# Token statistics taken in the convolution stage, and gate rows written from ScalarE's queue, in a four-layer image network

## Chip, core and metric

The kernel runs on one core of a Trainium2 chip. The metric is the time of one execution on the device, in microseconds (us); less is better. The engines are TensorE (PE: matrix products and transposes), VectorE (DVE), ScalarE (ACT), GpSimd (POOL) and SyncE (SP, which here only issues transfers). Each runs its own instruction stream in order; they meet at semaphores.

## What is computed

An image batch x of shape (4, 64, 128, 128), fp32, goes through four layers, each a mixing block over the image and a feed-forward block over its 65,536 tokens of 64 channels, both with a normalisation ahead and a residual around them. The change touches layer 1 (both blocks) and the feed-forward block of layer 3:

```python
x = x + L1_conv(_ln_c(x)); t = tokens(x); t = t + L1_ffn(_ln_t(t))
...
t = tokens(x); t = t + L3_ffn(_ln_t(t))          # same function, other weights

def L1_conv(x, gamma, beta, w_lbp, w_1x1, b_1x1):
    xn = batch_norm(x, gamma, beta)               # mean, variance over batch and image
    y = relu(conv3x3(xn, w_lbp)) + x
    return einsum('bchw,oc->bohw', y, w_1x1) + b_1x1

def ffn(x, router_w, router_b, expert_w, expert_b):   # 8 experts, 2 per token
    p, i = top_k(softmax(x @ router_w + router_b), 2)
    p = p / p.sum(-1)
    all = einsum('bnd,edc->bnec', x, expert_w) + expert_b
    return einsum('bnk,bnkc->bnc', p, take_along_axis(all, i))

def _ln_t(v):                                      # over the 64 channels of a token
    return (v - mean(v)) / sqrt(var(v) + 1e-5)
```

## The kernel before

build_program emits the stages one after another; each has its own on-chip tiles and one instruction stream per engine, and the next stage opens when all engines have ended. The names of tiles in the profile carry the stage's prefix.

**Convolution stage** (stage_conv_bn, prefix cb). Its first phase normalises all tokens and turns them to channel-major strips u. Its second walks 64 strips of 8 image rows in pairs. For each pair TensorE makes the 3x3 convolution (L1444, L1458); VectorE adds relu of it to u and writes y (add_relu, L1341 for the even strip, two halves L1345 for the odd); TensorE multiplies y by the 1x1 weights, which turns it back to tokens (mix, L1469); VectorE adds the old tokens, to which POOL has added the bias (L1263), into h (add_rest, L1353). SP loads old tokens (L1200) and stores new ones (L1205), a tile of 1024 tokens each, in the layout tokens_by_pair. mix of a pair comes a half pair after its convolution, between the next pair's straight and beside products. ScalarE normalises the strips ahead (L1401, L1404).

**Routed stage** (stage_top2_ffn, prefix t) runs twice: t1 in layer 1, where tiles of tokens are loaded from and stored to memory (rows is None), and t3 in layer 3, where the tokens lie on chip in passes and POOL joins a residual column to them (L1704) and the finished image is stored by SP in 32 pieces (L1655). Both make 32 beats; a beat works on four tiles in different steps. Its steps for a beat n: VectorE takes the statistics of n+3 (stats: 16 x L1727, five small operations), ScalarE their root (L1808, L1811), VectorE the shift (norm, L1739). ScalarE normalises n+2 (normalise, 2 x 8 x L1819), TensorE turns it (L1910), ScalarE copies it to ht (L1827), TensorE makes router logits and turns them (L1918, L1925), VectorE picks two experts (route, L1743 to L1759) and, after an exponential (L1841), makes the gates (gate, L1763 to L1768). TensorE turns the gates of n+1 (L1932), ScalarE copies them to gs (save_gates, L1837), SP writes them to memory as rows (keep_gates, L1634), and, when that has landed, SP reads each row back, spread to 64 partitions (spread_gates, 8 transfers of 512 KB into z, L1642). VectorE multiplies z by ht (weigh, L1775), TensorE sums over the experts (mix, L1942) and adds the residual (L1948, L1951), ScalarE copies out (finish, L1853), and SP stores (t1: L1647; t3: four times 8 image stores).

The order on ScalarE in a beat is written out: normalise(n+2, 0), save_gates(n+1), normalise(n+2, 1), copies of the turned halves, logits, root(n+3), mixed result, finish. The order on SP in a beat is load(n+4) (t1) or load_columns(2n+9) (t3), store(n-1), keep_gates(n+1), spread_gates(n+1, 0), load_columns(2n+10), spread_gates(n+1, 1). `since` waits for a semaphore only from a positive count on.

Of the kernel before, what the change touches and what calls it, by code (L numbers as in the profile page):

```python
# [1080 lines left out]
def stage_conv_bn(nc, tok, gamma, beta, w_lbp, w_1x1, b_1x1):  # L1081
# [8 lines left out]
    with ExitStack() as ctx:  # L1090
# [25 lines left out]
        y = a.sb("y", [128, 2, R, P2])  # L1116
        pH = [a.ps(f"pH{i}", [128, 512]) for i in range(2)]
# [34 lines left out]
        sum_ready = a.sem("sum_ready")  # L1152
        stored = [a.sem(f"stored{i}") for i in range(2)]
# [23 lines left out]
        def tokens_by_pair(n):  # L1177
            return tok[bass.ds(n * TILE, TILE), :].rearrange("(q p j) c -> p q (j c)", p=128, j=2)

        @block.sync  # L1180
        def _(sp):
# [16 lines left out]
            def load(n, par):  # L1198
                sp.wait_ge(sum_ready, n + 1)
                sp.dma_start(xs[:, par, :, :].rearrange("p (q j) c -> p q (j c)", j=2),  # L1200
                             tokens_by_pair(n)).then_inc(r_in[par], 16)

            def store(n, par):
                sp.wait_ge(sum_ready, n + 3)
                sp.dma_start(tokens_by_pair(n), h[:, par, :, :].rearrange(  # L1205
                    "p (q j) c -> p q (j c)", j=2)).then_inc(stored[par], 16)
# [62 lines left out]
        def _(dve):  # L1269
# [61 lines left out]
            def add_relu(n):  # L1331
# [30 lines left out]
        @block.scalar  # L1362
        def _(act):
# [43 lines left out]

            for n in range(B * NT):
                normalise(n)

# [93 lines left out]
def stage_top2_ffn(nc, stage, tok, router_w, router_b, expert_w, expert_b, gate_rows, rows=None, image=None):  # L1504
# [13 lines left out]
    with ExitStack() as ctx:  # L1518
# [91 lines left out]
        def _(sp):  # L1610
# [21 lines left out]
            def keep_gates(m):  # L1632
                sp.wait_ge(gs_saved, m + 1)
# [1224 lines left out]
```

## Time and profile before

| | |
|---|---|
| median of 3 runs | 6325.05 us (6322.73 to 6328.15) |
| profiled execution | 6345.72 us, its span 6343.9 us |
| busy in the span | PE 5095.5, DVE 4296.8, ACT 3437.0, POOL 1150.9 us |
| convolution stage, second phase | about 1456 to 1778 us |
| t1 | about 1782 to 2446 us |
| t3 | about 5563 to 6344 us |

All times on the time axis are from the start of the span of the one profiled execution. A timeline row begins with start and duration; "x8" joins eight like instructions that follow each other; a bracket holds the idle time of that engine before the row and what ended it. SPq is SP's queue issuing transfers; such a row's duration is the issue, not the transfer. PEclk is the TensorE clock that the throttle granted, 1.00 being full speed (2.4 GHz) and 0.50 the lower level (1.2 GHz). Instructions whose work is hidden beside another engine cost nothing; what counts in a stage is the wait that ends last.

### The profile page before, as it was taken

To read this page: it belongs to the slowest core of one execution; us is meant where nothing else is said; L and a number is where in the kernel's file an instruction comes from. 1 tells how busy PE (TensorE), PEld (TensorE's weight loads), DVE (VectorE), ACT (ScalarE), POOL (GpSimd) and SP (SyncE) were. 2 spreads that over 40 slices of the span, in tenths; PEclk is the share of its full clock that TensorE was granted. 3 is DMA by queue.
4 is the path that set the end of the run, shared out by engine and by line. 5 is a ranking of instruction groups with operands and counts; after the bars stand their busy time and mean duration, and the time that the engine had idled before them with its cause. 6 is when DMAs were issued, how large, how long until landed. Compare 5 with 4: busy or idle time off the path is not lost. (4 is left out here: it accounts for less than half of the span.)

```text
span 6343.9 us, 130904 instructions
## 1 busy us (share of the span) xinstructions
PE 5095.5 (80%) x47166; PEld 3310.4 (52%) x47166; DVE 4296.8 (68%) x9648; ACT 3437.0 (54%) x6857; POOL 1150.9 (18%) x1068
## 2 busy tenths in 40 slices
PE   7887886548968885799969998308999999948887
PEld 5665664224533332699969994104555555523332
DVE  7896887793358887622223447697777777768886
ACT  5664665465546564522243225366676767645554
POOL 2332332162200003400000000131111112221110
PEclk9998998758989996799989999659999999979999
DMA  1111113232358884200000124237666666547777
GB/s 35 36 32 35 37 37 84 67 104 83 108 164 277 276 281 159 69 0 0 0 0 0 67 102 132 66 98 96 81 81 81 81 81 81 68 137 238 238 241 223
DMA packets 794229, 646.31 MB, mean 102 GB/s; under 512 B 496551, under 2 KB 644199, under 8 KB 793779
## 3 DMA queue, kind: packets, MB, share of 16 engines
q1 hardware_dynamic: 792755, 639.06, 40.7%
q8 instruction: 307, 5.03, 0.3%
q0 software_dynamic: 1024, 1.05, 0.1%
q14 instruction: 143, 1.17, 0.1%
HBM read 549.78 MB, written 90.20 MB: 101 GB/s over the span
## 5 line engine op out<-in xcount | busy, mean ns | idle before, releaser
L2365 PE MATMUL sw_pC<-sw_row,sw_wc 128*128 128x128 f32 x10160 | 1159.3, 274 | 56.2 <-DVE sw_row L2240 54.9
L2365 PEld LDWEIGHTS sw_pC<-sw_row,sw_wc 128*128 128x128 f32 x10160 | 1148.0, 191 | 58.3 <-DVE sw_row L2240 55.5
L2799 PE MATMUL sp_pC<-sp_work,sp_bands 64*64 64x512 f32 (+11 forms) x14592 | 986.0, 428 | 44.2 <-issue 44.2
L2228 DVE SCALAR_TENSOR_TENSOR sw_row<-sw_pC,sw_y 128x128 f32<-128x128 f32 x1016 | 337.7, 332 | 792.2 <-PE sw_pC L2365 792.2
L2799 PEld LDWEIGHTS sp_pC<-sp_work,sp_bands 64*64 64x64 f32 x14592 | 602.1, 133 | 431.4 <-issue 365.3
L2738 ACT ACTIVATE sp_pC<-sp_pC,sp_par 128x512 f32<-128x512 f32 x832 | 598.4, 741 | 371.1 <-PE sp_pC L2799 348.0
L1775 DVE TENSOR_TENSOR t_z<-t_z,t_ht 128x1024 f32<-128x1024 f32 x512 | 628.4, 1267 | 93.8 <-DMA t_z<-gate_rows 91.7
L1942 PE MATMUL t_pO<-t_z,t_ew 128*64 128x512 f32 x2048 | 518.6, 626 | 100.0 <-DVE t_z L1775 98.3
L2297 ACT ACTIVATE sw_y<-sw_row 128x128 f32 (+1 forms) x762 | 265.6, 349 | 592.7 <-DVE sw_row L2228 592.7
L2695 DVE TENSOR_TENSOR sp_work<-sp_work,sp_pC 128x512 f32<-128x512 f32 x512 | 351.5, 688 | 170.1 <-ACT sp_pC L2738 169.6
L308 POOL TENSOR_TENSOR wa_sc<-wa_sc,wa_sm 128x1024 f32<-128x1024 f32 x128 | 243.8, 1904 | 665.7 <-DVE wa_sm L397 665.7
L1910 PE MATMUL t_pT<-t_ident,t_h 128*128 128x128 f32 x1024 | 158.5, 304 | 199.5 <-ACT t_h L1819 109.5
L1942 PEld LDWEIGHTS t_pO<-t_z,t_ew 128*64 128x64 f32 x2048 | 125.3, 139 | 349.0 <-DVE t_z L1775 185.5
L2738 ACT ACTIVATE sp_side<-sp_pC,sp_par 64x512 f32<-64x512 f32 x384 | 297.3, 774 | 7.5
L2600 POOL COPY sp_bands<-sp_bands 128x1536 f32<-128x1536 f32 x96 | 141.1, 1470 | 813.3 <-PE sp_pC L2799 774.6
L1910 PEld LDWEIGHTS t_pT<-t_ident,t_h 128*128 128x128 f32 x1024 | 125.7, 155 | 271.4 <-ACT t_h L1819 160.0
L2812 PE MATMUL sp_pC<-passes,sp_roll 128*128 128x512 f32 x128 | 59.0, 616 | 219.0 <-ACT passes L2729 219.0
L821 POOL MEMSET c_eps<- 128x1 f32 x2 | 0.2, 102 | 1256.0 <-POOLq L56 1256.0
L2693 DVE TENSOR_TENSOR sp_work<-sp_work,sp_pC 64x512 f32<-64x512 f32 x320 | 219.6, 686 | 7.1
L1704 POOL TENSOR_TENSOR passes<-passes,t_xs 128x512 f32<-128x512 f32 x64 | 118.1, 1846 | 558.1 <-DMA t_xs<-tokens 558.1
L1846 ACT ACTIVATE t_oc<-t_pO 128x512 f32<-128x512 f32 x128 | 76.3, 596 | 261.2 <-PE t_pO L1942 261.2
L2330 ACT ACTIVATE sw_packed<-sw_row 128x128 f32<-128x128 f32 x256 | 79.5, 311 | 249.2 <-DVE sw_row L2228 249.2
(375 smaller groups left out, 9736.8 us busy)
## 6 DMA issues: line engine op xcount, KB each, us to landing
t_z<-gate_rows SPq DMA_DIRECT2D x512, 512.0 KB, 8.0
sp_bands<-windows SPq DMA_DIRECT2D x128, 512.0 KB
c_spent<-tokens SPq DMA_DIRECT2D x128, 256.0 KB, 2.7
cb_xs<-tokens SPq DMA_DIRECT2D x128, 256.0 KB, 2.9
wa_xs<-in_x SPq DMA_DIRECT2D x64, 256.0 KB, 2.9
tokens<-wa_xt SPq DMA_DIRECT2D x128, 128.0 KB, 1.9
tokens<-cb_h SPq DMA_DIRECT2D x64, 256.0 KB, 2.7
t_xs<-tokens SPq DMA_DIRECT2D x32, 512.0 KB, 11.5
```

Of the source, the lines that this page charges most:

```text
L308: pool.tensor_tensor(p, p, r, ALU.mult).then_inc(probs_ready, 1)
L1775: dve.tensor_tensor(z[:, i, q, :], z[:, i, q, :], ht[:, m.k % HR, i, :], ALU.mult).then_inc(z_ready, 1)
L1910: ins = pe.transpose(pT[s][:, 128 * j:128 * j + 128], h[:, i, 4 * s + j, :, :].rearrange("p c d -> p (c d)"), ident[:, :])
L1942: ins = pe.matmul(pO[i][64 * s:64 * s + 64, :], ew[:, q, :], z[:, i, q, 512 * s:512 * s + 512], start=(q == 0), stop=(q == 3))
L2228: dve.scalar_tensor_tensor(row[par][c][:, :, PAD:PAD + P2], pC[c][:, 0:2 * P2].rearrange("p (b w) -> p b w", b=2), 0.0, line(sweep, c, i), ...
L2297: act.activation(line(sweep, c, i), row[par][c][:, :, PAD:PAD + P2], ACT.Copy).then_inc(saved[c], 1)
L2365: ins = pe.matmul(pC[c][:, 0:2 * P2], wc[:, sweep, m, :], row[1 - par][c][:, :, m:m + P2], start=(m == 0), stop=(m == 4))
L2600: pool.tensor_copy(dst, src[:, :, ::-1]).then_inc(band_ready, 1)
L2693: ins = dve.tensor_tensor(new[halves[here], :], old[halves[here], :], rel[halves[1 - here], :], ALU.add)
L2695: return dve.tensor_tensor(new, old, rel, ALU.add)
L2738: return act.activation(out[rows_out, :], pC[q][rows_in, :], ACT.Relu, bias=par[rows_in, c, BI + i:BI + i + 1], scale=par[rows_in, c, SC + ...
L2799: ins = pe.matmul(out[halves[to], :, low * lo:low * hi], band[halves[k], (NV * g + j) % BANDS, q, AT[k][tap], :], v[halves[k], :, low * at ...
```

## The change

Three edits. In the convolution stage the tokens are loaded and stored with eight consecutive tokens on a partition (tokens_of), the layout of t1; for that y is written with the token's place k outermost. VectorE then takes the statistics of each stored tile there, ahead of the next pair's add_rest, with variance, root and shift once for 16 strips, into a tile `carried` that stays on chip for t1. In t1 statistics, root and shift are dropped; its normalise waits for the tile's load and uses `carried`. In t1 and t3, the gate rows' write is issued by ScalarE right after the copy that it writes, and SP's order in a beat puts spread_gates(n+1, 0) ahead of the tile load and the store.

```diff
-        def tokens_by_pair(n):
-            return tok[bass.ds(n * TILE, TILE), :].rearrange("(q p j) c -> p q (j c)", p=128, j=2)
+        def tokens_of(n):
+            return tok[bass.ds(n * TILE, TILE), :].rearrange("(p j) c -> p (j c)", j=TS)
+
+        def statistics_of(b):
+            return slice(b * NT * TS, (b + 1) * NT * TS)
...
-                out = y[:, par, :, :].rearrange("p r w -> p (r w)")
+                out = y[:, par, :, :].rearrange("p r w -> p (r w)").rearrange("p (k q) -> p q k", k=TS // 2)
                 before = u[:, :, :, :].rearrange("p b r w -> p (b r w)")[:, n * R * P2:(n + 1) * R * P2]
+                before = before.rearrange("p (q k) -> p q k", k=TS // 2)
+                conv = p[:, :].rearrange("p (q k) -> p q k", k=TS // 2)
                 if par == 0:
-                    ins = dve.scalar_tensor_tensor(out, p[:, :], 0.0, before, ALU.max, ALU.add)
+                    ins = dve.scalar_tensor_tensor(out, conv, 0.0, before, ALU.max, ALU.add)
                 else:
                     for half in range(2):
                         here, there = slice(64 * half, 64 * half + 64), slice(64 - 64 * half, 128 - 64 * half)
-                        ins = dve.scalar_tensor_tensor(out[here, :], p[there, :], 0.0, before[here, :], ALU.max, ALU.add)
+                        ins = dve.scalar_tensor_tensor(out[here], conv[there], 0.0, before[here], ALU.max, ALU.add)
                 ins.then_inc(y_ready, 1)
...
+                if n >= 2:
+                    dve.wait_ge(next_seen, n - 1)
                 dve.wait_ge(stored[par], 8 * (n - par) + 16)
                 dve.tensor_tensor(h[:, par, :, :].rearrange("p t c -> p (t c)"),
                                   xs[:, par, :, :].rearrange("p t c -> p (t c)"), pY[par][:, :], ALU.add).then_inc(sum_ready, 1)
 
+            def next_stats(n):
+
+                dve.wait_ge(sum_ready, n + 3)
+                for j in range(TS):
+                    ins = dve.bn_stats(token_stats[:, n // NT % 2, TS * (n % NT) + j, :], h[:, n % 2, j, :])
+                ins.then_inc(next_seen, 1)
+
+            def next_variance(b):
+
+                at = statistics_of(b)
+                dve.wait_ge(next_seen, NT * (b + 1))
+                half = [token_stats[:, b % 2, :, k] for k in range(6)]
+                apart, rest = parts[:, 0, :], parts[:, 1, :]
+                dve.tensor_tensor(apart, half[1], half[4], ALU.subtract)
+                dve.tensor_tensor(carried[:, 1, at], half[1], half[4], ALU.add)
+                link(dve.tensor_tensor(rest, half[2], half[5], ALU.add))
+                link(dve.scalar_tensor_tensor(carried[:, 0, at], apart, C / 4.0, apart, ALU.mult, ALU.mult))
+                dve.tensor_tensor(carried[:, 0, at], carried[:, 0, at], rest, ALU.add).then_inc(next_var, 1)
+
+            def next_shift(b):
+
+                at = statistics_of(b)
+                dve.wait_ge(next_rstd, b + 1)
+                dve.scalar_tensor_tensor(carried[:, 1, at], carried[:, 1, at], -0.5, carried[:, 0, at], ALU.mult, ALU.mult)
+
             for n in range(0, B * NT, 2):
                 add_relu(n)
                 add_relu(n + 1)
+                if n > 0:
+                    next_stats(n - 2)
+                    next_stats(n - 1)
+                if n > 0 and n % NT == 0:
+                    next_variance(n // NT - 1)
+                if n > NT and n % NT == 8:
+                    next_shift(n // NT - 1)
                 add_rest(n)
                 add_rest(n + 1)
+            next_stats(B * NT - 2)
+            next_stats(B * NT - 1)
+            next_variance(B - 1)
+            next_shift(B - 1)
...
+            def next_root(b):
+
+                v = carried[:, 0, statistics_of(b)]
+                act.wait_ge(next_var, b + 1)
+                act.activation(v, v, ACT.Ln, bias=eps[:, 1:2], scale=1.0 / C).then_inc(next_log, 1)
+                act.wait_ge(next_log, b + 1)
+                act.activation(v, v, ACT.Exp, scale=-0.5).then_inc(next_rstd, 1)
+
             for n in range(B * NT):
                 normalise(n)
+                if n > NT and n % NT == 7:
+                    next_root(n // NT - 1)
+            next_root(B - 1)
...
-            def keep_gates(m):
-                sp.wait_ge(gs_saved, m + 1)
-                sp.dma_start(gate_rows[m, :, :].rearrange("e (j p) -> (e j) p", p=128),
-                             gs[:, m % 2, :]).then_inc(g_out[m % 2], 16)
-
             def spread_gates(m, i):
                 sp.wait_ge(g_out[m % 2], 16 * (m // 2 + 1))
                 for q in range(4):
             if rows is not None:
                 for t in range(7):
                     load_columns(t)
-            keep_gates(0)
             for i in range(2):
                 spread_gates(0, i)
                 if rows is not None:
                     load_columns(7 + i)
             for n in range(NB):
+                if rows is not None and 2 * n + 9 < 2 * NB:
+                    load_columns(2 * n + 9)
+                if n + 1 < NB:
+                    spread_gates(n + 1, 0)
                 if rows is None and XR <= n + 4 < NB:
                     load(n + 4)
-                if rows is not None and 2 * n + 9 < 2 * NB:
-                    load_columns(2 * n + 9)
                 if n > 0:
                     store(n - 1)
-                if n + 1 < NB:
-                    keep_gates(n + 1)
-                    spread_gates(n + 1, 0)
                 if rows is not None and 2 * n + 10 < 2 * NB:
...
+                if carried is None and n.plus(3).within(NB):
                     stats(n.plus(3))
                 weigh(n, 1, range(4))
                 if n.plus(2).within(NB):
                     route(n.plus(2))
-                if n.plus(3).within(NB):
+                if carried is None and n.plus(3).within(NB):
                     norm(n.plus(3))
 
             first = Beat(0, 0, 0)
-            for i in range(2):
-                stats(first.plus(i))
-                norm(first.plus(i))
-            stats(first.plus(2))
+            if carried is None:
+                for i in range(2):
+                    stats(first.plus(i))
+                    norm(first.plus(i))
+                stats(first.plus(2))
             route(first)
-            norm(first.plus(2))
+            if carried is None:
+                norm(first.plus(2))
             gate(first)
             route(first.plus(1))
             over_beats(dve, beat)
...
             def normalise(m, i):
-                act.wait_ge(scale_ready, m.n + 1)
+                if carried is None:
+                    act.wait_ge(scale_ready, m.n + 1)
+                    scale, shift = (v[:, m.k % 2, TS * i:TS * i + TS] for v in (sd, nm))
+                else:
+                    act.wait_ge(x_in[m.k], m.q * 16 + 16)
+                    scale, shift = (carried[:, k, J * m.n + TS * i:J * m.n + TS * i + TS] for k in range(2))
                 since(act, h_turned, 4 * m.n + 2 * i - 2)
                 x = x_of(m, i)
                 for j in range(TS):
-                    at = slice(TS * i + j, TS * i + j + 1)
                     ins = act.activation(h[:, i, j, 0:C - 1, :], bcast(x[:, j, 0:C - 1], C - 1, 2), ACT.Identity,
-                                         bias=nm[:, m.k % 2, at], scale=sd[:, m.k % 2, at])
+                                         bias=shift[:, j:j + 1], scale=scale[:, j:j + 1])
                 ins.then_inc(h_ready, 1)
...
                 act.activation(gs[:, m.k % 2, :], pT[0][:, 0:128], ACT.Copy).then_inc(gs_saved, 1)
+                act.wait_ge(gs_saved, m.n + 1)
+                act.dma_start(gate_rows.rearrange("m e t -> m (e t)")[bass.ds(m.n, 1), :].rearrange(
+                    "a (k p) -> (a k) p", p=128), gs[:, m.k % 2, :]).then_inc(g_out[m.k % 2], 16)
...
+    with nc.sbuf_tensor("carried", [128, 2, B * S // 128], FP32) as carried:
+        stage_conv_bn(nc, tok, *(p["L1_conv_" + n] for n in ("gamma", "beta", "w_lbp", "w_1x1", "b_1x1")), carried)
+        stage_top2_ffn(nc, "t1", tok, *(p["L1_ffn_" + n] for n in ("router_w", "router_b", "expert_w", "expert_b")), gate_rows,
+                       carried=carried)
```

## Rows read from the trace of the kernel before

**Rows 1.** Busy us by stretch: length, PE, PEld, DVE, ACT, POOL; clock, DMA, GB/s.
```profile
1456.00:1777.00 321.00, 319.19 (x1664) 159.83 (x1664) 109.57 (x159) 167.08 (x204) 78.74 (x63) 0.99 0.36 102
1864.13:2396.28 532.15, 451.69 (x2492) 201.52 (x2492) 473.79 (x1373) 329.27 (x841) 0.00 (x0) 0.98 0.82 278
5707.65:5794.76 87.11, 75.48 (x358) 32.50 (x356) 77.56 (x205) 51.06 (x121) 15.67 (x9) 0.90 0.70 221
6064.33:6146.14 81.81, 69.18 (x358) 28.95 (x356) 75.24 (x205) 49.78 (x121) 15.65 (x9) 1.00 0.77 239
```

**Rows 2.** Same view, gate copies (L1837) alone, t1's steady stretch.
```profile
1864.13:2396.28 532.15, 7.23 (x28) 0.98 0.82 278
```

**Rows 3.** One t1 beat's timeline: start, us, engine, line, operation, count [idle <-releaser].
```profile
1937.53 0.26 ACT L1837 ACTIVATE t_gs<-t_pT 128x128 f32<-128x128 f32 x1
1937.69 3.17 ACT L1819 ACTIVATE t_h<-t_xs,t_nm,t_sd 128x126 f32<-128x126 f32 x8
...
1941.48 1.06 PE L1910 MATMUL t_pT<-t_ident,t_h 128*128 128x128 f32 x8 [1.37 <-ACT t_ht L1827]
...
1955.88 0.26 ACT L1837 ACTIVATE t_gs<-t_pT 128x128 f32<-128x128 f32 x1
```

**Rows 4.** Waits of VectorE, 1840 to 2400: total us, times, longest.
```profile
DVE t_z L1775 <- DMA t_z<-gate_rows: 41.0, 62, 1.6
```

**Rows 5.** Timeline of one pair of strips, convolution loop.
```profile
1556.46 0.69 DVE L1341 SCALAR_TENSOR_TENSOR cb_y<-cb_pH,cb_u 128x512 f32<-128x512 f32 x1 [2.15 <-PE cb_pH L1458]
...
1557.19 1.39 DVE L1345 SCALAR_TENSOR_TENSOR cb_y<-cb_pH,cb_u 64x512 f32<-64x512 f32 x2
...
1561.50 1.95 PE L1469 MATMUL cb_pY<-cb_w,cb_y 128*128 128x128 f32 x16
...
1562.60 0.69 DVE L1353 TENSOR_TENSOR cb_h<-cb_xs,cb_pY 128x512 f32<-128x512 f32 x1 [4.02 <-PE cb_pY L1469]
```

**Rows 6.** Strided writes: source views (min/median/max ns), and a timeline row.
```profile
L1766 DVE TENSOR_TENSOR t_one<-t_one x64: 291/292/294, 1821.7 to 6294.6; 128x128 f32<-128x128 f32 x64
...
L1768 DVE TENSOR_TENSOR t_gates<-t_one,t_gt x64: 372/376/1807, 1822.0 to 6294.9; 128x128 f32<-128x128 f32 x64
...
4291.86 1.43 DVE L2671 TENSOR_TENSOR passes<-sp_work,sp_st 128x256 f32<-128x256 f32 x1
```

**Rows 7.** Timeline of the start of t1.
```profile
1796.08 2.13 DVE L1727 BATCH_NORM_STATS2 t_bs<-t_xs 128x6 f32<-128x64 f32 x16 [0.71 <-DMA t_xs<-tokens]
...
1799.93 3.17 ACT L1819 ACTIVATE t_h<-t_xs,t_nm,t_sd 128x126 f32<-128x126 f32 x8 [0.24 <-DVE t_nm L1739]
...
1820.93 3.16 ACT L1819 ACTIVATE t_h<-t_xs,t_nm,t_sd 128x126 f32<-128x126 f32 x8
```

**Rows 8.** Timeline of the convolution's end and t1's opening.
```profile
1777.43 0.69 DVE L1353 TENSOR_TENSOR cb_h<-cb_xs,cb_pY 128x512 f32<-128x512 f32 x1 [0.85 <-POOL cb_xs L1263]
...
1781.59 1.28 ACT L1803 ACT_TABLE_LOAD   x1 [22.33 <-PEq L56]
```

**Rows 9.** Source view of the gate write on SP's queue: durations in ns, landing in us.
```profile
L1634 SPq DMA_DIRECT2D gate_rows<-t_gs x64: 325/332/2185, 1832.6 to 6297.8; - x64
...
DMA to landing us min/median/max: 2.4/8.1/9.9
```

**Rows 10.** Timeline of two turns in t3, TensorE.
```profile
5777.11 1.94 PE L1910 MATMUL t_pT<-t_ident,t_h 128*128 128x128 f32 x8 [2.51 <-ACT t_ht L1827]
...
5798.46 1.06 PE L1910 MATMUL t_pT<-t_ident,t_h 128*128 128x128 f32 x8 [2.51 <-ACT t_ht L1827]
```

**Rows 11.** Timeline of the end of t1.
```profile
2423.91 1.23 DVE L1775 TENSOR_TENSOR t_z<-t_z,t_ht 128x1024 f32<-128x1024 f32 x1 [4.14 <-DMA t_z<-gate_rows]
```

**Rows 12.** Timeline of a beat of t3 with image stores.
```profile
5812.12 15.75 SPq L1655 DMA_DIRECT2D out<-passes  x8
...
5827.91 2.19 SPq L1634 DMA_DIRECT2D gate_rows<-t_gs  x1
...
5836.11 1.23 DVE L1775 TENSOR_TENSOR t_z<-t_z,t_ht 128x1024 f32<-128x1024 f32 x1 [9.62 <-DMA t_z<-gate_rows]
```

More of the change, by code:

```diff
@@ L1078, in _, with stage_conv_bn @@
             ins.then_inc(summed, 1)
-def stage_conv_bn(nc, tok, gamma, beta, w_lbp, w_1x1, b_1x1):
+def stage_conv_bn(nc, tok, gamma, beta, w_lbp, w_1x1, b_1x1, carried):
     TS = 8
@@ L1116, in stage_conv_bn @@
         y = a.sb("y", [128, 2, R, P2])
+        token_stats = a.sb("token_stats", [128, 2, NT * TS, 6])
+        parts = a.sb("parts", [128, 2, NT * TS])
         pH = [a.ps(f"pH{i}", [128, 512]) for i in range(2)]
@@ L1152, in stage_conv_bn @@
         sum_ready = a.sem("sum_ready")
+        next_seen = a.sem("next_seen")
+        next_var = a.sem("next_var")
+        next_log = a.sem("next_log")
+        next_rstd = a.sem("next_rstd")
         stored = [a.sem(f"stored{i}") for i in range(2)]
@@ L1199, in load @@
                 sp.wait_ge(sum_ready, n + 1)
-                sp.dma_start(xs[:, par, :, :].rearrange("p (q j) c -> p q (j c)", j=2),
-                             tokens_by_pair(n)).then_inc(r_in[par], 16)
+                sp.dma_start(xs[:, par, :, :].rearrange("p j c -> p (j c)"), tokens_of(n)).then_inc(r_in[par], 16)
             def store(n, par):
                 sp.wait_ge(sum_ready, n + 3)
-                sp.dma_start(tokens_by_pair(n), h[:, par, :, :].rearrange(
-                    "p (q j) c -> p q (j c)", j=2)).then_inc(stored[par], 16)
+                sp.dma_start(tokens_of(n), h[:, par, :, :].rearrange("p j c -> p (j c)")).then_inc(stored[par], 16)
             load(0, 0)
@@ L1501, in since, with stage_top2_ffn @@
         eng.wait_ge(sem, value)
-def stage_top2_ffn(nc, stage, tok, router_w, router_b, expert_w, expert_b, gate_rows, rows=None, image=None):
+def stage_top2_ffn(nc, stage, tok, router_w, router_b, expert_w, expert_b, gate_rows, carried=None, rows=None, image=None):
     E = 8
@@ L1719, in stats @@
             def stats(m):
-                if rows is None:
-                    dve.wait_ge(x_in[m.k], m.q * 16 + 16)
-                else:
-                    dve.wait_ge(joined, 2 * m.n + 2)
+                dve.wait_ge(joined, 2 * m.n + 2)
                 for i in range(2):
@@ L1870, in beat @@
                         save_logits(m, i)
-                if n.plus(3).within(NB):
+                if carried is None and n.plus(3).within(NB):
                     root(n.plus(3))
@@ L1888, in _ @@
             first = Beat(0, 0, 0)
-            root(first)
+            if carried is None:
+                root(first)
             prepare(first)
-            root(first.plus(1))
-            root(first.plus(2))
+            if carried is None:
+                root(first.plus(1))
+                root(first.plus(2))
             gap(first)
@@ L2829, in build_program @@
     stage_choice_ffn(nc, "c0", tok, *(p["L0_ffn_" + n] for n in ("gate_w", "gate_b", "weight1", "weight2")))
-    stage_conv_bn(nc, tok, *(p["L1_conv_" + n] for n in ("gamma", "beta", "w_lbp", "w_1x1", "b_1x1")))
-    stage_top2_ffn(nc, "t1", tok, *(p["L1_ffn_" + n] for n in ("router_w", "router_b", "expert_w", "expert_b")), gate_rows)
+    with nc.sbuf_tensor("carried", [128, 2, B * S // 128], FP32) as carried:
+        stage_conv_bn(nc, tok, *(p["L1_conv_" + n] for n in ("gamma", "beta", "w_lbp", "w_1x1", "b_1x1")), carried)
+        stage_top2_ffn(nc, "t1", tok, *(p["L1_ffn_" + n] for n in ("router_w", "router_b", "expert_w", "expert_b")), gate_rows,
+                       carried=carried)
     stage_sweeps(nc, tok, [p["L2_conv_kernel_" + n] for n in ("td", "dt", "lr", "rl")])
```

1 line of the change is left out of this document (removed).

## The prediction

> **What bounds the kernel now.** I read, in this order, the busy times by stretch, the gate copies and one beat of the first routed stage (t1), VectorE's waits there, one pair of strips in the convolution stage, and then the ends of the stages and the last routed stage (t3). The stretches [rows 1] show different limits. In the convolution loop TensorE is busy for 319.19 of 321.00 us: nothing matters there unless TensorE is made to wait. In t1 no engine is full: TensorE 451.69, VectorE 473.79 and ScalarE 329.27 of 532.15 us. That stretch holds 28 gate copies [rows 2], 532.15 / 28 = 19.01 us a beat. What sets the beat is a loop through two engines [rows 3]: from one gate copy (L1837) to the next is 1955.88 - 1937.53 = 18.35 us. In between ScalarE normalises the second half of a tile (L1819, 1937.69) and only then copies the turned first half; TensorE, which waited 1.37 us for just that copy, turns the second half (L1910, 1941.48) and goes on through logits, mix and residual; ScalarE's copy of the result and the next normalisation follow. 13 of the 28 beats take 18.35 or 18.36 us and none is shorter. A limit from VectorE or from transfers would not repeat so exactly. The excess over it is (19.01 - 18.35) x 28 = 18.4 us, and it goes with VectorE's waits for the spread gates, 41.0 us in 62 waits, 1.6 at most [rows 4].
>
> In t3 the same loop runs; its undisturbed beat is 81.81 / 4 = 20.45 us at a granted clock of 1.00 [rows 1].
>
> **The change part by part.**
>
> **Convolution loop.** VectorE's work for a pair is 0.69 + 1.39 us for y, then 4.02 us idle until TensorE's mix ends, then two sums [rows 5]. Three edits go there. First, y is written with 512 bytes between neighbouring elements. No row has this write. The nearest is the gates' write (64 bytes apart), 376 ns against 292 for as many elements written in place [rows 6]: 84 / 128 = 0.66 ns an element, +0.34 us for 512. The far one is the write into passes, 1.43 us for 256 elements with POOL at work beside it [rows 6]: 2.86 for 512, +2.2. I take the near one, because POOL's bias sum runs beside y already and the second line still takes two times 0.69. Then y is done at 1556.46 + 3.1 = 1559.6, and the mix starts at 1561.50: no cost. Second, 16 statistics for the pair before, 2.13 us [rows 7]: until 1561.8, ahead of the sum at 1562.60. Three times some 0.9 us of small operations joins them; that just fits, and at worst delays 3 pairs of 32 by a fraction of a microsecond. Third, token transfers in pieces of 2 KB in place of 512 bytes: TensorE doesn't wait for them, 0. A gain is excluded, since TensorE is full; without cover, each microsecond that y is late costs 32.
>
> **Convolution tail.** After the last sum, 1777.43 + 0.69 = 1778.12, the stage only waits for its stores, and t1 opens at 1781.59 [rows 8]. Now the statistics (2.13) and the small operations, root and shift follow; in t1 these lie between 1796.08 + 2.13 = 1798.21 and 1799.93 [rows 7], 1.7 us. That ends at 1782.0, +0.4, and up to 3.0 with a table load of 1.28 us ahead of each of the two functions [rows 8]. **+2**.
>
> **Start of t1.** The first normalisation starts when its tile has landed, 1796.08, and not at 1799.93 [rows 7]: -3.9. The second tile's, at 1820.93, is held by the first routing, which VectorE takes up only after the third tile's statistics, 2.13 + 0.9 = 3.0. Less a little for the routing's own start: **-6.6** in all, -3.9 if only the first shows.
>
> **Steady t1, 30 beats.** VectorE loses some 3 us a beat. It isn't in the loop, so this alone gives 0. The gate write moves from SP to ScalarE, into the loop. Today the second normalisation starts 0.16 us after the copy starts [rows 3]. Now ScalarE must see the copy end (0.26), issue the write, and go on; behind its wait stand the second normalisation and the turned tile, for which TensorE already waits. No row has a transfer issued by ScalarE; SP's issue of the same write takes 0.33 us in the median, 2.19 at most [rows 9]. 0.26 + 0.33 - 0.16 = 0.43, with a little for dispatch **+0.5** a beat; bounds 0.3 (issue partly overlapped) and 0.75, so 9 to 22, taken **+15**. Against that, the write leaves at once, on a queue without the 512 KB spreads; it takes 8.1 us to land today in the median, 2.4 at least [rows 9]. Five microseconds sooner are more than VectorE's longest wait, 1.6, so the **-18.4** goes (bound: 0, if it lands no sooner). On SP the spreads now pass tile load and store, which leave some 6 us later; a tile is loaded two beats ahead of its use, so 0. What is late next: TensorE, on ScalarE alone. It is busy 451.69 / 28 = 16.1 us a beat, so its pauses add up to 18.85 - 16.1 = 2.7, now in one piece. t3 has such a piece: of 20 waits of 2.2 to 2.5 us at L1910, 12 are followed by a turn of 1.3 to 1.94 us, the others by one of 1.06 [rows 10], and the granted clock over four such beats is 0.90, not 1.00 [rows 1]; these four take 87.11 us, not 81.81. The turns alone lose 0.4 us a beat on average. For t1 I take **+12** (0 to 29, none or 0.96 in each). Sum of the steady part: +8.6.
>
> The Trainium skill speaks against the sooner landing: "DMA: Bandwidth & Descriptors", section "Issuing engines are not separate DMA queues", says that transfers started by different engines run on the same 16 DMA engines and interleave, and that only issuing time is saved. By it the -18.4 would be lost and the forecast be 18 us higher; the trace, in which one queue issues all these transfers, bears it out neither way. That outcome is rival D.
>
> **End of t1.** With nothing left to normalise, the gates' way is the path: the last beat's first product waits 4.14 us for its spread [rows 11]. Landing sooner: **-4** (0 to -6).
>
> **t3, 30 beats.** Its statistics stay. The issue costs **+15** as above (9 to 22). Three times SP issues eight image stores first, 15.75 us from 5812.12; the gate write leaves at 5827.91, and VectorE waits 9.62 us until 5836.11 [rows 12]. These beats and the next are 25 us over the rest in all. Now the write and the first four spreads go ahead of the stores; the other four still follow them, at some 5838, for a need at about 5836, and with the landing VectorE stalls 4 to 6 us. **-13** (-6 to -20). TensorE's one wait grows from 2.5 to 3.0: **+4** for the clock (0 to 14). Sum +6.
>
> **Total.** +2 - 6.6 + 8.6 - 4 + 6 = **+6**: 6345.7 + 6 = 6352 for the profiled execution. That one was 20.7 us above the median of the runs shown, 6325.05, and no row places the difference, so the same offset is taken: **6331**.
>
> **The rivals.**
> B, faster: ScalarE's issue costs 0.3 and no further clock is lost. t1 9 - 18.4 - 6.6 - 4, t3 9 - 20, convolution +1: -30, 6295. For it: four t3 beats at full clock in spite of such waits [rows 1]; against: the 12 others.
> C, slower: TensorE's one long wait lowers the clock in every beat of both stages; t1 29 in place of 12, t3 14 in place of 4: 6 + 27 = +33, 6358. It decides, as slower, from about three beats in four.
> D, the write lands no sooner from ScalarE's queue, so the change doesn't do what it says: 18.4 and 4 stay, the stores give back 10, the clock costs 4 in t3: 2 - 6.6 + 15 + 15 - 10 + 4 = +19, 6345.
> E, y is written at 2.86 us an operation. It is then ready at 1565.1, where the mix's second half wants it at 1562.5: 2.6 x 32 = +83, 6414 with the rest. It decides from 2.0 us an operation. Against: POOL beside y costs nothing today.
> F, VectorE is t1's limit after all; its 473.79 / 28 = 16.9 us a beat fall by 3, and the beat goes to TensorE's 16.1: 30 x 2.9 = -87, 6240. Against: the constant 18.35.
>
> **How the numbers follow.** Chances: forecast 0.41 (its own range 6314 to 6344), B 0.24, C 0.18, D 0.10, E 0.04, F 0.03. A difference under 0.2%, 12.6 us, can't be told from no change here. Faster: B nearly whole, F, a little of the forecast, 0.27. Slower: C, most of D, E and a part of the forecast, 0.34. Same 0.39. The range leaves out E, F and the outer parts of B and C: 6290 to 6364.
>
> **What would show it.** Right: beats of 18.85 us in t1 without waits of VectorE for gates, a wait near 2.7 at L1910, t3 beats of 20.95, an unchanged convolution pair, t1's first normalisation right on the landing. Wrong: t1 beats of 18.35 or less (issue hidden, or F), turns of 1.94 us in nearly all beats (C), waits for the spread gates still there (D), L1341 over 2 us (E).

## Result and the profile after

The changed kernel takes 6382.56 us (median, 6378.87 to 6386.21); the kernel before 6324.82 us beside it. The ratio is 1.0091, 95% interval 1.0073 to 1.0108: 58 us slower, where 6331 was forecast and the range ended at 6364. Its profiled execution took 6386.2 us, its span is 6384.4 us.

I split both spans at the opening of the stages (the first row of POOL in each) and take two profiles of before, the one shown above and a second one from the experiments:

| stretch | before | before, second profile | after |
|---|---|---|---|
| up to the convolution stage | 1271.9 | 1267.5 | 1272.5 |
| convolution stage | 509.7 | 509.8 | 515.4 |
| t1 | 665.6 | 662.6 | 683.3 |
| the stages between (unchanged) | 3116.2 | 3114.3 | 3115.7 |
| t3 | 780.4 | 778.4 | 797.5 |

The stages without a change agree within 5 us. The rest is +5.6 us in the convolution stage, +18 to +21 in t1 and +17 to +19 in t3. How t1 lost it is seen in the busy times by stretch (columns as in [rows 1]; the second row is the stretch from the third gate copy over 28 beats):

```profile
1450.00:1780.00 330.00, 320.51 (x1668) 160.83 (x1668) 218.44 (x682) 180.79 (x222) 81.38 (x64) 0.98 0.32 99
1866.47:2417.76 551.29, 458.81 (x2494) 214.80 (x2492) 402.73 (x757) 323.88 (x786) 0.00 (x0) 0.93 0.83 269
```

The 28 beats take 551.29 us, 19.69 each, against 532.15 [rows 1]. VectorE is relieved (402.73 us for 473.79), and the granted clock is 0.93, not 0.98. The timeline of one such beat, in the order of [rows 3] (ACTq is ScalarE's queue issuing a transfer):

```profile
1945.17 0.26 ACT L1891 ACTIVATE t_gs<-t_pT 128x128 f32<-128x128 f32 x1
1945.46 0.33 ACTq L1893 DMA_DIRECT2D gate_rows<-t_gs  x1
...
1945.89 3.18 ACT L1873 ACTIVATE t_h<-t_xs,carried 128x126 f32<-128x126 f32 x8 [0.46 <-ACT t_gs L1891]
...
1949.69 1.06 PE L1969 MATMUL t_pT<-t_ident,t_h 128*128 128x128 f32 x8 [3.05 <-ACT t_ht L1881]
...
1950.69 1.95 PE L1977 MATMUL t_pX<-t_ht,t_rw 128*32 128x256 f32 x16
...
1965.11 0.26 ACT L1891 ACTIVATE t_gs<-t_pT 128x128 f32<-128x128 f32 x1
```

The copy starts at 1945.17 and the second normalisation at 1945.89, after 0.72 us where it was 0.16: the copy's 0.26, and 0.46 us in which ScalarE sees the copy end and issues the write (0.33). TensorE turns the first half, has nothing else to do, and waits 3.05 us in one piece. The products after it then take 1.95 us for 16 of 256 columns, which take two times 0.64 at full clock (L1977, from 2069.56 us in the beat shown next). So the beat is 1965.11 - 1945.17 = 19.94 us. A beat without a loss of clock is 18.92:

```profile
2064.05 0.26 ACT L1891 ACTIVATE t_gs<-t_pT 128x128 f32<-128x128 f32 x1
...
2082.97 0.26 ACT L1891 ACTIVATE t_gs<-t_pT 128x128 f32<-128x128 f32 x1
```

That is 18.35 + 0.57. 21 of the 28 beats are more than half a microsecond above it. The write itself lands sooner than from SP's queue (source view; compare [rows 9]):

```profile
L1893 ACTq DMA_DIRECT2D gate_rows<-t_gs x64: 326/326/352, 1835.1 to 6338.2; - x64
...
DMA to landing us min/median/max: 2.6/4.6/6.6
```

Who waits in t1 has changed as well (waits between 1860 and 2420: total us, times, longest; first a row of before, then two of the changed kernel):

```profile
PE t_pO L1942 <- DVE t_z L1775: 47.1, 55, 1.6
```

```profile
DVE t_z L1823 <- DMA t_z<-gate_rows: 59.9, 70, 2.6
...
PE t_pT L1969 <- ACT t_ht L1881: 85.4, 28, 3.1
```

VectorE still waits for the spread gates, for 59.9 us where it was 40.2 in the same window before. But TensorE, which waited 47.1 us for the tiles that VectorE weighs, has no such wait any more. It waits for ScalarE's copy alone, once in every beat.

### The profile page after: what moved, and what is told of

Its sections match the earlier page's. It is cut to its first block and busy times, and to the rows that moved or that the text cites. A ratio compares the mean times of both kernels' runs of the same rounds, so it can differ in the third digit from the quotient of the medians.

```text
span 6384.4 us, 130690 instructions
## 1 busy us (share of the span) xinstructions
PE 5113.4 (80%) x47166; PEld 3326.0 (52%) x47166; DVE 4324.8 (68%) x9480; ACT 3445.5 (54%) x6809; POOL 1147.4 (18%) x1068
## 3 DMA queue, kind: packets, MB, share of 16 engines
q1 hardware_dynamic: 734387, 634.86, 40.2%
## 5 line engine op out<-in xcount | busy, mean ns | idle before, releaser
L1873 ACT ACTIVATE t_h<-t_xs,carried 128x126 f32<-128x126 f32 x512 | 202.8, 480 | 27.8 <-DMA t_xs<-tokens 14.0
```

Source lines behind the costliest of these rows:

```text
L1873: ins = act.activation(h[:, i, j, 0:C - 1, :], bcast(x[:, j, 0:C - 1], C - 1, 2), ACT.Identity, bias=shift[:, j:j + 1], scale=scale[:, j:j ...
```

## Experiments

Two theories were set against each other. **A**: ScalarE's issue lengthens the loop by 0.57 us, and TensorE's single longer wait lowers its clock in most beats. **B**: VectorE's relief is what gathers TensorE's pauses into one; the issue costs its own time and no more. Ratios are to the kernel before on the same chip; 0.1% is 6.3 us, and two kernels whose intervals overlap are not told apart by them. The columns t1 and t3 are from one profile each: the time of 28 beats from the third gate copy on, and the shortest beat. One and the same code differs there from profile to profile: t1 took 551.3 us (after) and 556.6 (after, stores last), t3 took 615.2 and 614.3 (before) and 605.1 (before with carried statistics). So less than some 5 us in t1 and 10 in t3 is not read as an effect.

| kernel | ratio (interval) | t1 | shortest | t3 | shortest |
|---|---|---|---|---|---|
| before | 1 | 532.2 | 18.35 | 615.2 | 20.41 |
| before, second profile | | 532.4 | 18.34 | 614.3 | 20.44 |
| after | 1.0091 (1.0073 to 1.0108) | 551.3 | 18.92 | 631.2 | 20.99 |
| write on SP | 1.0034 (1.0022 to 1.0045) | 545.1 | 18.35 | 609.9 | 20.43 |
| before with write on ScalarE | 1.0074 (1.0054 to 1.0094) | 549.7 | 18.91 | 634.1 | 21.01 |
| before with carried statistics | 1.0005 (0.9995 to 1.0016) | 535.5 | 18.35 | 605.1 | 20.44 |
| after with idle turns | 1.0024 (1.0015 to 1.0034) | 532.6 | 18.91 | 618.0 | 21.02 |
| after, write later | 1.0107 (1.0090 to 1.0124) | 560.8 | 18.35 | 634.6 | 20.42 |
| before, residual early | 0.9978 (0.9968 to 0.9988) | 532.0 | 16.98 | 593.6 | 19.20 |
| carried, residual early | 0.9985 (0.9975 to 0.9995) | 532.9 | 16.87 | 597.0 | 18.69 |
| after, residual early | 0.9940 (0.9920 to 0.9960) | 507.1 | 17.20 | 598.8 | 18.66 |
| after, stores last | 1.0050 (1.0033 to 1.0067) | 556.6 | 18.92 | 618.0 | 21.01 |
| after, early, idle turns, stores last | 0.9963 (0.9949 to 0.9977) | 512.8 | 17.52 | 609.9 | 19.55 |
| the same without carried statistics | 0.9961 (0.9948 to 0.9973) | 515.4 | 17.84 | 609.9 | 19.29 |

### One part alone: the write, the statistics

**Write back on SP**, the rest as changed:

```diff
+            keep_gates(m) on SP, as before, just ahead of spread_gates(m, 0)
-                act.wait_ge(gs_saved, m.n + 1)
-                act.dma_start(gate_rows...)
```

> The changed kernel with only the gate write put back on SP, issued there just ahead of the spreads; carried statistics and the new order of SP's queue stay. In the changed kernel the shortest t1 beat is 18.92 us (18.35 before), and most beats are 19.7 to 20.1. Theory A (ScalarE's issue of 0.57 us lengthens the loop, and the longer single wait of TensorE, 3.05 us, lowers its clock in most beats): the shortest beat goes back to 18.35, the wait at the second turn falls to about 2.5, fewer beats run at the lower clock; 30 to 34 us come back from the issue in both stages and 10 to 20 more from the clock: 6330 to 6340. Theory B (only VectorE's relief merges TensorE's pauses, the issue costs its 0.57 and nothing else): t1 beats still 0.8 above their shortest on average: 6345 to 6352.

1.0034: 36 us of the 58 are back, the shortest beats are 18.35 and 20.43 again. But the average t1 beat is 19.47, and 22 us above before is what B expected (20 to 27), not A (5 to 15). The reason is neither's. With the write on SP and the new order, it lands late, VectorE waits for the spreads and TensorE for VectorE (source view of the write; waits in t1, 1860 to 2420):

```profile
L1692 SPq DMA_DIRECT2D gate_rows<-t_gs x64: 320/337/610, 1829.6 to 6302.4; - x64
...
DMA to landing us min/median/max: 2.4/8.9/10.5
```

```profile
DVE t_z L1830 <- DMA t_z<-gate_rows: 115.6, 96, 4.1
...
PE t_pO L2005 <- DVE t_z L1830: 43.2, 57, 1.4
```

SP's new order is part of this: the kernel with carried statistics and SP's old order, shown below, differs from this one in that order alone and stands at 1.0005, with 535.5 us in t1 for 545.1.

**Only the write on ScalarE** (and SP's order), statistics in t1 as before:

> The kernel before with only the gate write moved to ScalarE and SP's order changed; statistics stay in t1, the convolution stage is as before. Theory A: the issue is 0.57 us in 60 beats, 34 us, and TensorE's wait at the second turn is long in most beats whatever VectorE does: 6365 to 6380. Theory B: with VectorE still taking statistics, TensorE's pauses stay split in t1, so its beats stay near 18.92 to 19.2: +34, less 10 from the stores of t3: 6340 to 6352.

1.0074, by itself four fifths of the loss (the interval overlaps that of the whole change), and the same wait of TensorE as with the whole change, though VectorE still takes its statistics:

```profile
1940.36 0.33 ACTq L1832 DMA_DIRECT2D gate_rows<-t_gs  x1
...
1944.59 1.94 PE L1906 MATMUL t_pT<-t_ident,t_h 128*128 128x128 f32 x8 [3.05 <-ACT t_ht L1820]
```

B falls here: t1 is 549.7 us, not some 530, and VectorE's relief isn't needed for the long wait.

**Only the statistics carried**, write on SP, SP's order as before:

> The kernel before with only the statistics carried from the convolution stage (its layout, its strided write of y included); gate write on SP and SP's order as before. The convolution stage ends 6 us later, t1 starts 4 us less late: +2. Theory A: t1 beats as before, 18.35 at the shortest and about 19.0 on average: 6322 to 6332. Theory B: VectorE's relief alone gathers TensorE's pauses in one of 2.2 to 2.5 us, the clock falls in half the beats, and t1 is 10 to 15 us longer: 6335 to 6342.

1.0005: no difference that can be told, as A expected. B's lengthening of TensorE's pause at the second turn isn't shown by it (waits of TensorE in t1, 1860 to 2420: before, before in its second profile, this kernel):

```profile
PE t_pT L1910 <- ACT t_ht L1827: 23.0, 28, 2.3
```

```profile
PE t_pT L1910 <- ACT t_ht L1827: 32.3, 29, 2.5
```

```profile
PE t_pT L1973 <- ACT t_ht L1888: 38.4, 27, 2.5
```

38.4 us is more than 23.0, but the two profiles of before are 9 us apart themselves. The beats come to 19.13 us on average against 19.01: nothing is gained by the relief. So far the write on ScalarE is the loss, and the question is how much of it is the issue and how much the clock.

### The clock

**Idle turns in the pause**, on the changed kernel (their results are overwritten):

```diff
                 if due:
-                    for i in range(2):
-                        turn(m, i)
+                    turn(m, 0)
+                    since(pe, y_ready, 2 * n.n)
+                    for _ in range(4):
+                        for j in range(4):
+                            pe.transpose(pY[1][:, 128 * j:128 * j + 128], ident[:, :], ident[:, :])
+                    turn(m, 1)
                     route(m)
```

> The changed kernel with 16 idle turns of a constant tile (128x128, about 2.1 us, results overwritten later) on TensorE between the two turns of a beat, where it waits 3.05 us for ScalarE. If the lower clock comes from that wait, the turns after it take 1.06 us in all beats, t1 beats come to 18.92 (551 to 530 us for 28 of them), and t3 gains as much or a little less: 6338 to 6350. If the long beats come from the transfers or from VectorE, nothing changes: 6380 to 6386; if the added turns are themselves late, 6390 or more.

1.0024: useless work gives back 42 of the 58 us. TensorE's timeline shows the idle turns (L2036), a wait of 1.30 left of 3.05, and all later products at full clock; the window of t1 has a granted clock of 1.00:

```profile
1942.10 1.91 PE L2036 MATMUL t_pY<-t_ident 128*128 128x128 f32 x16
1945.32 1.06 PE L1969 MATMUL t_pT<-t_ident,t_h 128*128 128x128 f32 x8 [1.30 <-ACT t_ht L1881]
...
1947.18 0.64 PE L1977 MATMUL t_pX<-t_ht,t_rw 128*32 128x256 f32 x8 [0.23 <-ACT t_ht L1881]
```

```profile
1866.00:2396.00 530.00, 482.75 (x2930) 248.44 (x2928) 396.42 (x755) 316.92 (x779) 0.00 (x0) 1.00 0.84 275
```

27 of 28 beats are within half a microsecond of 18.91; in the changed kernel 7 were. So in t1 the clock costs 551.3 - 532.6 = 18.7 us (some 5 more against the other profile of the same t1), and the issue 28 x 0.57 = 16.0. That is theory A. VectorE's waits for the spreads are no shorter here, 92.8 us, and cost next to nothing: TensorE waits 6.4 us for weighed tiles.

**The write issued later by ScalarE**, just ahead of its wait for TensorE's mix:

```diff
     save_gates(m):
-        act.wait_ge(gs_saved, m.n + 1)
-        act.dma_start(gate_rows...)
     beat(n):
             if carried is None and n.plus(3).within(NB):
                 root(n.plus(3))
+            if n.plus(1).within(NB):
+                send_gates(n.plus(1))
             save_mixed(n, 1)
```

> The changed kernel with ScalarE issuing the gate write some 7 us later in its beat, just ahead of its wait for TensorE's mix, and no longer between the two normalisations. If the place of the issue in the loop is what costs, t1's shortest beat returns from 18.92 to 18.35, t3's from 21.03 to 20.45, TensorE's wait at the second turn from 3.05 to about 2.5, and the clock falls in fewer beats: 6335 to 6355, as with the write on SP. If the issue costs ScalarE its time wherever it stands, or if a later landing makes VectorE wait instead: 6375 to 6390.

1.0107, the slowest of all, and above both ranges. The first half of the expectation came true: the shortest beats are 18.35 and 20.42, and TensorE's wait at the second turn is nearly gone (7.2 us in all; 85.4 in the changed kernel). But the second did too, VectorE waits for the spreads, and TensorE 67.0 us for VectorE:

```profile
DVE t_z L1823 <- DMA t_z<-gate_rows: 134.0, 121, 3.8
...
PE t_pT L1974 <- ACT t_ht L1881: 7.2, 17, 1.0
```

The way of the gates (copy, write, landing, spread) is a second limit just beside the loop. The write has to leave early; early on ScalarE costs the loop, and early on SP it lands late.

**Before, profiled again.**

> The kernel before, unchanged, profiled a second time: its first profiled execution took 6345.7 us, 20.7 above its median. If the excess lies in beats at the lower clock in the routed stages, this profile shows t1 or t3 shorter (the kernel with carried statistics alone, whose t3 is the same code, took 605.1 us for 28 beats of t3, against 615.2) and the rest of the stages within 3 us; if it lies elsewhere, other stages differ.

6334.4 us, 3 above the median of the runs beside it. t1 and t3 have 532.4 and 614.3 us in 28 beats, as in the first profile. What made the first profile 20.7 above its runs isn't in the routed beats; of 11 us between the two, 4.4 lie ahead of the convolution stage and the rest is spread. It stays open.

### Useful work in the pause

**Residual products early**, on the kernel before: both x products (L1948) are made between the two turns, and only the products of oc at the end.

```diff
                 if due:
-                    for i in range(2):
-                        turn(m, i)
+                    turn(m, 0)
+                    for i in range(2):
+                        add_x(n, i)      # pY[i] = x, start=True, stop=False
+                    turn(m, 1)
                     route(m)
...
```

> The kernel before, with TensorE's two residual products (L1948, 0.56 us each) moved from the end of the beat into its wait between the two turns, in t1 and t3: useful work in the pause. If TensorE's pause is what lowers the clock, fewer beats take the long form, and the loop loses up to 1 us of TensorE's chain too: t1 beats 17.3 to 18.0 at the shortest, t3 19.5 to 20.0, together 30 to 60 us: 6270 to 6300. If the pause doesn't matter and VectorE or the transfers take over as the limit: 6315 to 6330.

0.9978, some 14 us where 25 to 55 were expected. The shortest beat falls by 1.4 us, to 16.98, but t1 as a whole stays at 532.0, as in before. The timeline of one beat says why: the gate write leaves SP's queue at 2010.83, the first spread of it at 2020.18, and VectorE waits.

```profile
2010.83 0.33 SPq L1634 DMA_DIRECT2D gate_rows<-t_gs  x1
...
2014.83 1.88 PE L1948 MATMUL t_pY<-t_xs,t_ident 128*128 128x512 f32 x4
...
2020.18 5.82 SPq L1642 DMA_DIRECT2D t_z<-gate_rows  x8
...
2026.20 1.23 DVE L1775 TENSOR_TENSOR t_z<-t_z,t_ht 128x1024 f32<-128x1024 f32 x1 [0.67 <-DMA t_z<-gate_rows]
```

**The same with carried statistics:**

> The same move of the residual products, together with the statistics carried from the convolution stage, the gate write on SP and SP's order as before. If VectorE limits t1 once TensorE's pause is used, the 3 us a beat that it is relieved of count now: t1 10 to 25 us below the same move without carried statistics, less 2 in the convolution stage: 6255 to 6290. If VectorE isn't in the way even then, within 5 us of that kernel.

0.9985, t1 532.9, not the 6255 to 6290 of a VectorE in the way: relieving it of 3 us a beat changes nothing even here. It isn't t1's limit.

**The same on the changed kernel**, with the write on ScalarE:

> The changed kernel with TensorE's two residual products moved into its wait between the two turns. With the write on ScalarE the gates land sooner, so the loop alone should set the beat: shortest t1 beat 18.92 - 1.0 = 17.9 or less, t3 about 20.0, and the part of the pause that is left (3.05 - 1.0) lowers the clock in fewer beats: 6300 to 6335, below the kernel before. If the gates' way (write, spread, weighing) sets the beat as it did with the write on SP and the products moved, t1 stays near 19.0 on average: 6335 to 6355.

0.9940 (0.9920 to 0.9960), 38 us faster than before, more than expected, and by the ratios 96 faster than the change as made. t1 is 507.1 us, 25 less than with the same move, the write on SP and SP's old order: once TensorE's pause is used, the sooner way of the gates pays. How much of it is the queue and how much SP's order wasn't tried apart. Busy time by stretch, clock 0.99:

```profile
1860.00:2360.00 500.00, 437.58 (x2456) 194.34 (x2454) 390.83 (x739) 320.26 (x780) 0.00 (x0) 0.99 0.88 292
```

**Stores behind both halves of the spreads** in t3, on the changed kernel:

> The changed kernel with SP's image stores of t3 behind both halves of the spread gates instead of between them. In the changed kernel the three beats with stores still take 28.8, 27.0 and 27.5 us, since the second half of the spreads waits behind 17.5 us of stores. If that is the reason, those beats fall to 21 to 23 and 15 to 20 us come back: 6360 to 6370. If the stores' own transfers slow the spreads, or the delay only moves to the next beat's columns, 6378 to 6388.

1.0050: by the ratios 26 us come back, by the two profiled spans 15. t3 falls from 631.2 to 618.0 us. The beats with stores are 22.4 to 24.0 us, not 27.0 to 28.8. With the beats behind them they give back 7.2 us; the other 6 lie in 22 beats without stores, which is no more than the same code differs by. SP's row of the second half now stands ahead of the stores:

```profile
5847.20 3.90 SPq L1695 DMA_DIRECT2D t_z<-gate_rows  x4
...
5851.15 17.29 SPq L1708 DMA_DIRECT2D out<-passes  x8
```

**All of it, with fewer idle turns,** and **the same without carried statistics:**

> The changed kernel with both: residual products early, 8 idle turns (1.06 us) ahead of them so that TensorE's wait is nearly full, and the image stores behind the spreads. If the clock follows the pause, all turns take 1.06 us, t1 beats 17.9 to 18.1 without exceptions, t3 20.0: t1 45, t3 50 us below the changed kernel: 6275 to 6300. If the idle turns make TensorE late: 6310 or more.

> The same three edits on the kernel before with the write on ScalarE, but with the statistics taken in t1: it tells what carrying them is worth once the loop is short. If VectorE (16.9 us a beat with statistics, 13.9 without) is out of the way at 18 us, it stands within 5 us of the version with carried statistics; if it is in the way, 15 to 40 us above it.

0.9963 and 0.9961. The first gains 23 us where 25 to 50 were expected; the second stands beside it, as expected of a VectorE out of the way. No gain over the early residual alone: the shortest t1 beat is 0.3 to 0.6 us longer than its 17.20. In that kernel TensorE waited 0.4 us in all at the second turn of t1, so the idle turns had no pause to fill and make TensorE late. Both edits without the idle turns weren't tried. The two kernels here can't be told apart: carrying the statistics is worth nothing that shows.

## Why the prediction was wrong

The mechanism was named: loop, issue on ScalarE, one long wait, lower clock. Rival C, at 0.18, had it in about three beats in four, and 21 of 28 are slower; but C's time, 6358, is 25 us short too. What failed is the size of the terms, nearly all in one direction. In order of size: the offset carried over from the first profile (17 us), the gain booked for t3's stores (9, outside its bounds of -6 to -20), the clock in t1 (7, inside its bounds), the end of t1 (5), the convolution tail (4) and the start of t1 (3). With the offset right, the forecast would have been 6348, still 34 us short.

| term | forecast | measured |
|---|---|---|
| convolution stage | +2 | +5.6 |
| start of t1 | -6.6 | -3.9 |
| t1: issue | +15 | +16.0 (28 beats) |
| t1: what the waits for gates cost the beat | -18.4 | about -15 |
| t1: clock | +12 | +18.7 |
| end of t1 | -4 | +0.8 |
| t3: issue | +15 | +16.0 (28 beats) |
| t3: stores | -13 | about -4 |
| t3: clock | +4 | about +4 (what is left of +16) |
| offset to the median | as before | 17 us off |

**Convolution loop: right.** The strided write costs 0.34 to 0.40 us an operation more, 0.38 in the median and near the 0.34 of the near row, and is covered; the mix still follows every 9.87 us. Timeline of a pair, to be laid beside [rows 5]:

```profile
1557.17 1.06 DVE L1350 SCALAR_TENSOR_TENSOR cb_y<-cb_pH,cb_u 128x512 f32<-128x512 f32 x1 [1.60 <-PE cb_pH L1516]
...
1558.26 2.14 DVE L1354 SCALAR_TENSOR_TENSOR cb_y<-cb_pH,cb_u 64x512 f32<-64x512 f32 x2
...
1560.43 2.12 DVE L1371 BATCH_NORM_STATS2 cb_token_stats<-cb_h 128x6 f32<-128x64 f32 x16
...
1562.21 1.95 PE L1527 MATMUL cb_pY<-cb_w,cb_y 128*128 128x128 f32 x16
...
1563.30 0.69 DVE L1364 TENSOR_TENSOR cb_h<-cb_xs,cb_pY 128x512 f32<-128x512 f32 x1 [0.74 <-PE cb_pY L1527]
```

VectorE now waits 0.74 us for the mix, where it was idle for 4.02.

**Convolution tail: under-sized.** I had let the statistics begin after the last sum of before. In the last pair nothing else runs on TensorE, so the covered work comes out into the open. Timeline from the last pair to the opening of t1:

```profile
1775.35 1.16 PE L1527 MATMUL cb_pY<-cb_w,cb_y 128*128 128x128 f32 x8 [1.23 <-DVE cb_y L1350]
...
1777.47 2.13 DVE L1371 BATCH_NORM_STATS2 cb_token_stats<-cb_h 128x6 f32<-128x64 f32 x16
...
1777.50 1.16 PE L1527 MATMUL cb_pY<-cb_w,cb_y 128*128 128x128 f32 x8 [0.99 <-DVE cb_y L1354]
1779.52 1.27 DVE L1364 TENSOR_TENSOR cb_h<-cb_xs,cb_pY 128x512 f32<-128x512 f32 x2
...
1784.93 1.28 ACT L1461 ACT_TABLE_LOAD   x1
...
1787.84 0.10 POOL L1746 MEMSET t_eps<- 128x1 f32 x1 [9.87 <-POOLq L56]
```

TensorE waits 1.23 and 0.99 us for the slower y (0.89 and 0.26 before), the statistics of the pair before (2.13) stand ahead of the last sums, and a table load of 1.28 lies between logarithm and exponential. Cover that holds in 31 pairs has to be looked at in the last one too.

**Start of t1: half the gain.** The first normalisation starts with its tile, as forecast. Counted from the opening of t1 it starts 3.0 us sooner than before, and the third gate copy comes 3.9 us sooner (2.5 against the second profile of before). But TensorE's first turn waits for another load, that of the expert bias, issued at 1802.63; what would be late next had not been asked:

```profile
1802.63 0.26 SPq L1715 DMA_DIRECT2D t_ew<-in_L_ffn_expert_b  x1
1803.17 3.17 ACT L1873 ACTIVATE t_h<-t_xs,carried 128x126 f32<-128x126 f32 x8 [14.05 <-DMA t_xs<-tokens]
...
1808.85 1.94 PE L1969 MATMUL t_pT<-t_ident,t_h 128*128 128x128 f32 x8 [30.20 <-DMA t_ew<-in_L_ffn_expert_b]
```

**Steady t1: the clock.** The issue was right (0.57 for 0.5). What the waits for the gates cost the beat went, as forecast: filled with idle turns, the changed kernel's t1 is 3.1 us above 28 x 18.91, where before was 18.4 above 28 x 18.35. But the sign named for it was wrong. The prediction asked for beats "without waits of VectorE for gates" and held waits that stay for rival D. They stayed, 59.9 us for 40.2, while TensorE's waits for VectorE went from 47.1 to none. With the write on ScalarE and the statistics still in t1, VectorE's waits are 8.3 us: relieved of 3 us a beat, it waits longer for the same gates at no cost. The step that failed in steady t1 is "I take +12 (0 to 29)" for the clock. From t3's waits of 2.2 to 2.5 us, 12 of 20 followed by slower turns, I took 0.4 us a beat for a longer wait; 3.05 us gave 21 of 28 beats and 0.67 a beat (18.7 / 28). The turn alone isn't the whole of what a lower clock costs: in the beat above it is at full clock and the products after it are slow. The rows that would have told more were the beats: four at a clock of 0.90 took 87.11 us and four at 1.00 took 81.81 [rows 1], 1.3 a beat.

**End of t1.** The last write lands 2.6 us after its issue, 4 us sooner than before, and the gain is gone all the same: from the last gate copy to the next stage it is 34.9 us, 34.1 before. VectorE's wait of 4.14 [rows 11] and the three after it (7.3 us in all) became five of 1.3 to 2.1 us for the spreads one by one (8.2 in all). Whether these are late through the tile stores beside them wasn't tried.

**t3: the stores.** In the forecast the second half of the spreads, behind the stores, was to stall VectorE for 4 to 6 us. It stalls for 7.40 in the beat that answers to [rows 12]:

```profile
5841.89 2.50 SPq L1695 DMA_DIRECT2D t_z<-gate_rows  x4
...
5844.44 17.54 SPq L1708 DMA_DIRECT2D out<-passes  x8
...
5862.02 3.92 SPq L1687 DMA_DIRECT2D t_xs<-tokens  x2
...
5866.04 2.69 SPq L1695 DMA_DIRECT2D t_z<-gate_rows  x4
...
5870.97 1.23 DVE L1823 TENSOR_TENSOR t_z<-t_z,t_ht 128x1024 f32<-128x1024 f32 x1 [7.40 <-DMA t_z<-gate_rows]
```

The wait of 9.62 became one of 7.40 a half beat later, because the stores take 17.54 us now and the columns' load (3.92) comes ahead of the spreads too. The three store beats and those behind them were 25.2 us above six plain ones (20.45 each, at full clock) and are 21.4 (21.0 each): 4 us gained for 13, 3 with the write alone on ScalarE, whose t3 is the same, and none with the idle turns (28.9 us above plain ones). With the stores behind both halves of the spreads these six beats are 14.2 us above plain ones: 11 us less than before, near the gain that the forecast had booked.

**Rival D** fell. The write lands 4.6 us after its issue in the median on ScalarE's queue and 8.9 with only the write put back on SP's; over all runs it is 2.0 to 6.4 and 7.1 to 8.9. The sentence of the Trainium skill that was weighed ("DMA: Bandwidth & Descriptors", section "Issuing engines are not separate DMA queues": only issuing time is saved) isn't borne out for such a write: changing the queue halved its landing, with the 16 engines as busy (share 0.83 against 0.84 in t1). That SP's spreads, which stand ahead of it on SP's queue, are the reason is argued and not shown.

**Offset.** I carried the 20.7 us between the profiled execution of before and its runs over to the changed kernel. Its profiled execution is only 3.6 above its median. By the spans the change is +40.5 us against the first profile of before and +51.8 against the second, and by the runs +57.7; so 6 to 17 us of it have no place in the table of stages. A single profile that stands off its runs by more than the question's size should not have been the base.

## What to carry to other kernels

Where two engines hand a beat to each other, an instruction put on the engine that the other waits for is paid in full (here 16.0 us in 28 beats) and may cost as much again through TensorE's clock (18.7). Look for the pause and put useful work into it before taking time from engines that don't set the beat. An engine's own wait is no sign of a loss; ask whether the engine that sets the beat waits for it. When an order is changed so that a transfer no longer waits behind another, follow all parts of it: the half left behind decides. And work that hides beside a full engine comes into the open in the last round of its loop.

## What the runs showed of the hardware

A constant wait of 3.05 us in every beat did not lower TensorE's clock in the same place each time: the second turn's duration goes 1.94, 1.77, 1.36, 1.06, 1.06 us through five beats and begins again after four or five, and 21 of 28 beats are longer. The first three, followed by 1949.69 above:

```profile
1889.91 1.94 PE L1969 MATMUL t_pT<-t_ident,t_h 128*128 128x128 f32 x8 [3.05 <-ACT t_ht L1881]
...
1909.86 1.77 PE L1969 MATMUL t_pT<-t_ident,t_h 128*128 128x128 f32 x8 [3.05 <-ACT t_ht L1881]
...
1929.91 1.36 PE L1969 MATMUL t_pT<-t_ident,t_h 128*128 128x128 f32 x8 [3.05 <-ACT t_ht L1881]
```

With 1.91 us of idle transposes in the wait the granted clock is 1.00 over t1's 530 us.

ScalarE's issue of a transfer takes 0.33 us, as on SP; with the wait for its own copy it delays the next activation by 0.57.
